# A fifth looked-up tile in the first block and one comparison for both features of a tile, in a one-core Trainium2 recommender kernel

## What is computed

```python
e = emb_tables[jnp.arange(F)[None, :], x]            # B=1024, F=32, D=64
gram = jnp.einsum('bid,bjd->bij', e, e)
cross = gram[:, iu, ju]                              # 496 pairs
h = jnp.concatenate([e.reshape(B, F * D), cross], axis=1)
h = jax.nn.relu(h @ W1 + b1)                         # 2544 -> 1024
h = jax.nn.relu(h @ W2 + b2)                         # -> 512
logits = h @ W3 + b3                                 # -> 1000
return jax.nn.sigmoid(logits)
```

## Time and profile before

| | us |
|---|---|
| median of 3 runs | 432.74 |
| lowest and highest | 430.98, 433.42 |
| the profiled execution, its own time | 431.43 |
| its span in the profile | 429.2 |
| PE busy in the span | 386.4 (90%) |
| DVE, ACT, POOL busy | 298.8, 248.0, 231.4 |

### The profile page before, as it was taken

One profiled execution on the slowest core, in us unless ns is written; L12 is line 12 of the kernel. 1 busy time (PEld: TensorE's weight loads), 2 busy tenths in 40 slices (PEclk: granted clock), 3 DMA queues, 4 the chain that ended last, 5 costly groups with the idle time before them and its releaser, 6 DMA issues.

```text
span 429.2 us, 7587 instructions
## 1 busy us (share of the span) xinstructions
PE 386.4 (90%) x2892; PEld 325.7 (76%) x2892; DVE 298.8 (70%) x568; ACT 248.0 (58%) x390; POOL 231.4 (54%) x246
## 2 busy tenths in 40 slices
PE   0887856896999998999999999999999999999996
PEld 0675744685789986788889888788889987788894
DVE  4999943484759966696579866878479767554652
ACT  3645533543667677536766676647667667444642
POOL 6887887064677777457757772457577700000000
PEclk9998898799899999999999999999999999999999
DMA  7765574069575777299874967497785864696512
GB/s 241 223 193 174 162 231 116 6 217 320 156 201 165 240 224 218 80 294 301 232 246 130 279 191 241 132 293 237 214 248 152 247 194 152 220 267 187 160 43 95
DMA packets 34451, 85.00 MB, mean 198 GB/s; under 512 B 6576, under 2 KB 13424, under 8 KB 33904
## 3 DMA queue, kind: packets, MB, share of 16 engines
q1 hardware_dynamic: 27504, 77.43, 57.1%
q0 software_dynamic: 6912, 7.09, 8.0%
HBM read 76.21 MB, written 8.29 MB: 197 GB/s over the span
## 4 chain that ended last, share of the span: by engine, by line
PE 55%; POOL 23%; issue 8%; DVE 5%; ACT 4%; DMA 3%; SPq 1%; DVEq 0%; POOLq 0%; ACTq 0%
POOL emb L429 21%; PE h1p L682 11%; PE h1p L684 11%; PE h1p L683 11%; PE misc L675 3%; PE misc L677 3%; PE misc L676 3%; PE misc L684 3%; PE misc L682 3%; PE misc L683 3%; DVE dg L587 2%; ACT wsplit L447 2%; PE misc L751 2%; POOL gap L420 2%; PE misc L729 2%
## 5 line engine op out<-in xcount | busy, mean ns | idle before, releaser
L429 POOL DMA_INDIRECT emb<-tables_dram,idx x216 | 222.3, 1029 | 112.0 <-issue 55.2
L563 DVE TENSOR_TENSOR wsplit<-wraw,wsplit 128x512 fp32r<-128x512 f32 (+1 forms) x224 | 143.7, 686 | 64.4 <-ACT wsplit L447 63.4
L447 ACT CAST wsplit<-wraw 128x1024 fp32r<-128x1024 f32 (+1 forms) x112 | 117.4, 1049 | 51.8 <-PE h1p L684 35.8
L682 PE MATMUL h1p<-wsplit,xhi 128*128 128x512 f32 x256 | 107.4, 419 | 3.6 <-DVE xlo L575 3.6
L683 PE MATMUL h1p<-wsplit,xlo 128*128 128x512 f32 x256 | 103.7, 405 | 0.0
L684 PE MATMUL h1p<-wsplit,xhi 128*128 128x512 f32 x256 | 103.6, 405 | 0.0
L682 PEld LDWEIGHTS h1p<-wsplit,xhi 128*128 128x128 f32 x256 | 50.0, 195 | 15.4 <-DVE wsplit L560 3.5
L684 PEld LDWEIGHTS h1p<-wsplit,xhi 128*128 128x128 f32 x256 | 49.9, 195 | 12.3
L683 PEld LDWEIGHTS h1p<-wsplit,xlo 128*128 128x128 f32 x256 | 50.2, 196 | 10.6
L637 DVE TENSOR_SCALAR hot<-xb,vals 128x256 fp32r<-128x256 int32 x160 | 51.9, 394 | 3.4 <-DMA xb<-xt_dram 3.4
L458 ACT COPY z<-misc 64x256 f32<-64x256 f32 x108 | 41.9, 388 | 13.8 <-DVE xlo L569 12.9
(11 more groups left out here) (50 smaller groups left out, 478.6 us busy)
## 6 DMA issues: line engine op xcount, KB each, us to landing
wraw<-w_dram SPq DMA_DIRECT2D x96, 512.0 KB, 4.6
wraw<-w_dram SPq DMA_DIRECT2D x16, 500.0 KB, 3.8
wraw<-tables_dram SPq DMA_DIRECT2D x10, 512.0 KB, 5.7
gram_scratch<-dg SPq DMA_DIRECT2D x4, 1024.0 KB, 5.0
out_dram<-res SPq DMA_DIRECT2D x16, 250.0 KB, 2.1
emb<-tables_dram,idx POOLq DMA_INDIRECT x216, 3.8
xb<-xt_dram SPq DMA_DIRECT2D x10, 256.0 KB, 5.5
gc<-gram_scratch SPq DMA_DIRECT2D x16, 64.0 KB, 4.6
```

The costliest lines, as they stand in the source:

```text
L429: nc.gpsimd.indirect_dma_start(emb[:, n % 2, k, t, f * D:(f + 1) * D], None, tables, bass.IndirectOffsetOnAxis(ap=idx[:, BT * n + t, 2 * k ...
L447: nc.scalar.copy(whi(u % RING, w), wraw[:, u % RAWS, 0:w]).then_inc(s_whi, 1)
L563: last = nc.vector.tensor_tensor(wlo(u % RING)[:, part], wraw[:, u % RAWS, part], whi(u % RING)[:, part].bitcast(fp32), ALU.subtract)
L682: nc.tensor.matmul(dst, hi, whi(slot)[:, cols], start=start, stop=False, skip_group_check=True)
```

## The change

In the first block tile 11 is looked up as well, so five tiles are looked up and eleven gathered (44 gathers instead of 48). The number of gathered tiles is then odd, and the last transpose of block 0 takes a single tile: `tiles_in(n, m)` gives one or two, and line 451, 569, 458 and 719's counterparts take half the width there. The first block's rounds are five, each with one look-up, one transpose and two emb steps, and the last transpose and emb 5 stand behind them. `products(0)` has emb 6 to 10 where it had 7 to 11. Tiles 2 and 3 of block 1 may be gathered once emb 8 of block 0 is done, not emb 11.

In all blocks the comparison is made for both features of a tile at once: eight instructions of 128x2x256 instead of sixteen of 128x256. Each of the eight signals by itself, and the look-up's products go chunk by chunk, both features of a chunk before the next chunk, each chunk waiting for its own signal. The "ones" items are therefore half as many; the one that is left stands where the first of the two stood.

```diff
-LOOKED_UP = ((12, 13, 14, 15),) + ((14, 15),) * (BLOCKS - 1)
+LOOKED_UP = ((11, 12, 13, 14, 15),) + ((14, 15),) * (BLOCKS - 1)
-        yield ("ones", 0, 1)
-        for k in range(4):
-            yield ("look", 0, 12 + k)
+        for k in range(5):
+            yield ("look", 0, 11 + k)
             yield ("tr", 0, k)
-            if k < 3:
-                yield ("ones", 0, 2 * k + 2)
-            yield from emb(0, 12 + k)
-            if k < 3:
-                yield ("ones", 0, 2 * k + 3)
-            yield from emb(0, k)
-        yield ("tr", 0, 4)
-        yield from emb(0, 4, 6)
+            if k < 4:
+                yield ("ones", 0, k + 1)
+            yield from emb(0, 11 + k, k)
         yield ("tr", 0, 5)
         yield from emb(0, 5)
...
-        yield from emb(n, *((7, 8) if n == 0 else (8,)))
+        yield from emb(n, *((6, 7) if n == 0 else (8,)))
         if more:
             yield ("ones", n + 1, 0)
-        yield from emb(n, 9)
-        if more:
-            yield ("ones", n + 1, 1)
-        yield from emb(n, 10)
+        yield from emb(n, *((8, 9) if n == 0 else (9, 10)))
         yield ("move", n)
...
-    done = (("emb", 0, 11), ("pair", 0, 0), ...
+    done = (("emb", 0, 8), ("pair", 0, 0), ...
...
+    def tiles_in(n, m):
+        return min(2, GATHERED[n] - 2 * m)
...
-                for k in range(2):
+                for k in range(tiles_in(n, m)):
...
-            def compare(h):
-                i, f = divmod(h, 2)
+            def compare(i):
                 dve.wait_ge(s_xb[i % 2], 16 * (i // 2 + 1))
-                if h >= HOTS:
-                    dve.wait_ge(s_used, used_after(*LOOKED[(h - HOTS) // 2]))
+                if i > 0:
+                    dve.wait_ge(s_used, used_after(*LOOKED[i - 1]))
                 for c in range(VC):
-                    last = nc.vector.tensor_scalar(hot[:, h % HOTS, c, :], xb[:, i % 2, f, :],
-                                                   vals[:, c:c + 1], None, ALU.is_equal)
-                last.then_inc(s_hot, 1)
+                    nc.vector.tensor_scalar(hot[:, :, c, :], xb[:, i % 2, :, :],
+                                            vals[:, c:c + 1], None, ALU.is_equal).then_inc(s_hot, 1)
...
-                for f in range(2):
-                    pe.wait_ge(s_hot, 2 * a + f + 1)
-                    for c in range(VC):
+                for c in range(VC):
+                    pe.wait_ge(s_hot, VC * a + c + 1)
+                    for f in range(2):
```

More of the change, by code:

```diff
@@ L651, in _ @@
                     looked_up_lo(n, k[0])
-                if kind == "ones" and (n, k[0]) > (0, 1):
-                    compare(2 * LOOK["look", n, LOOKED_UP[n][0]] + k[0])
+                if kind == "ones" and (n, k[0]) > (0, 0):
+                    compare(LOOK["look", n, LOOKED_UP[n][k[0]]])
                 if kind == "tr":
```

43 lines of the change are left out of this document (20 added, 23 removed).

## The result

The changed kernel takes 430.7 us in the median (20 runs, 428.28 to 434.67), the kernel before 432.64 beside it (20 runs, 430.26 to 435.62). The ratio is 0.9953, 95% interval 0.9932 to 0.9975: faster by 2.0 us, between 1.1 and 2.9. The sign was right, the size was not. The profiled execution took 430.89, its span 429.0.

What follows compares the result with a forecast made beforehand. POOL's gathers were taken to end the first block, then product reads through DRAM, then PE to bound. Terms: -7.0 at gram, +0.9 behind it, the rest 0, sum -6.1 us: 426.6 against the median 432.74, range 424.0 to 430.0.

Steps and rivals of the forecast that it cites:

- What bounds the kernel: POOL's gathers end block 0, product reads through DRAM follow, then PE bounds; earlier pair steps come off the end in full.
- Four gathers fewer: End of block 0: first 40 gathers untouched, transpose stays at 63.70, gram at 74.3 instead of 81.32, gain 7.0 us.
- The fifth look-up: Block 0's rounds: costs nothing; fifth result due at 57.9 by DVE alone, rounds of 10.0, copy must begin by 64.0.
- The wide comparison's own price: On DVE: a comparison of 512 columns takes 0.47 us, eight take 3.7, against 5.52 for a tile before.
- Behind gram: Block 0 after gram: table split and product reads issued 1.1 later; pair steps lose 0.9 us, between 0 and 2.2.
- Blocks 1 and 2: Reads there delayed by 1.2 us; block 1 has 1.75 of room and block 2 more, so cost 0.
- The two-input pace: Rival: wide comparison at two-input pace, eight take 4.9 us; gain 3.9, time 428.8; chance 0.14.
- the slower case: Rival: comparison of 512 costs at least two of 256; at 5.9 for eight, 2.6 us slower, 435.3; chance 0.06.
- POOL doesn't get faster: Rival in block 0: comparisons and gathers disturb each other, 44th gather some 6 us late; gain about 0.5, 432.2; chance 0.08.

Runs made afterwards that it cites:

- split_nogap: five_split without the small iotas that POOL runs after every two gathers of the first block; 423.06 us, ratio 0.9752 to the kernel before.
- five_split: The changed kernel with narrow comparisons of 128x256, one feature after the other at the two places as before; 427.64 us, ratio 0.9862 to the kernel before.
- experiment 5: POOL's first-block iotas, which fill a tile nothing reads, left out of the kernel before (0.9848), five_split (0.9752) and five_split with later-block wide comparisons (0.9803).
- only_five: The changed kernel with sixteen narrow comparisons at the place of the eight wide ones, iotas kept; 429.6 us, ratio 0.9896 to the kernel before.
- before_nogap: The kernel before without POOL's iotas in the first block; 425.2 us, ratio 0.9848 to the kernel before.
- hold_two: The changed kernel with SP's weight loads from emb 8 of block 0 on waiting for that block's last transpose; 430.33 us, ratio 0.9938.
- after_nogap: The changed kernel, wide comparisons everywhere they stood, without POOL's iotas in the first block; 431.21 us, ratio 0.9979 to the kernel before.
- only_cmp: The kernel before with the wide comparison alone, four tiles looked up in the first block as before; 436.35 us, ratio 1.0068 to the kernel before.
- wide_mid_nogap: The changed kernel without first-block iotas, each round's wide comparison there moved between the two emb steps; 430.07 us, ratio 0.9927 to the kernel before.
- hold: The changed kernel with SP's weight loads from emb 7 of block 0 on waiting for the transpose of tiles 8 and 9; 431.73 us, ratio 0.9950.
- before: The kernel before the change, unaltered; 432.64 us median beside the changed kernel.
- no_cmp: The changed kernel with seven of the eight comparisons of a look-up left out in four first-block rounds; 428.43 us, ratio 0.9874 to the kernel before.
- wide_mid: The changed kernel with each first-block round's wide comparison moved between its two emb steps, iotas kept; 429.25 us, ratio 0.9918 to the kernel before.

## Why the prediction was wrong in size

**What bounds the kernel** was read rightly. POOL's gathers end the first block, and every kernel here that brings gram forward and isn't held behind it is faster by about that: `split_nogap` starts gram 9.3 us earlier, and its ratio is 9.2 to 12.3 us off the total.

**Four gathers fewer** was right as a step of its own and failed on its first sentence: "The first 40 gathers are untouched ... so the transpose of tiles 8 and 9 stays at 63.70." Nothing in the program touches them; the wide comparison does, on the chip. The 40th gather is 2.5 us late, about 2 of it by gathers and iotas that run beside comparisons, and the loads that bunch behind the comparisons made its landing another 2.2 late: 4.7 of the 5.4 that gram missed. `five_split`, where the sentence holds (60.45, transpose at 63.40), gave 6.0 us. It did so with gram 4.8 earlier and not 7.0, since short waits and the low clock made 9.8 us, from one transpose to the next, of the 7.5 that the forecast had reckoned.

**The fifth look-up** at no cost came out, but not by its working. The limit was that the copy of the fifth result begins by 64.0. It begins later, on DVE's timeline of the changed kernel:

```profile
65.24 0.43 DVE L570 CAST xlo<-misc 64x256 fp32r<-64x256 f32 x1
```

PE never waits for it, because its transpose is itself at 68.39; had that stood at 63.70, PE would have waited. From the first such copy (16.70) to the fifth DVE's rounds take 12.1 us on average, not 10.0, since they follow PE, which waits for gathers. In `five_split`, where the transpose is in time, PE waits 0.78 us for the fifth copy and 1.88 for its comparisons at 61.97, and with the iotas gone as well the look-ups are what holds the block (experiment 5).

**The wide comparison's own price** was right (0.47 forecast, 0.477 measured; 3.66 for eight in a round, forecast 3.7). It was the wrong quantity to price. DVE's time isn't the bound, POOL's is, and the working costed the operation on the engine that runs it and not on the neighbour.

**Behind gram** 0.9 was reckoned and 0.4 measured (27.2 for 26.8), a term a little too large. **Blocks 1 and 2** at 0 was nearly right: the pair steps of block 1 don't wait, but PE's wait for gathered rows in block 1 grew from 1.5 to 2.4. In all eleven kernels with wide comparisons there it is 2.3 or 2.4; in those with narrow ones 1.4 to 1.8, and 2.3 in one, `only_five`.

**The rivals.** The two-input pace and the slower case fell with the 477 ns. "POOL doesn't get faster" came nearest, at 432.2 for the measured 430.7. Its price was 0.36 us on four gathers a round. Measured are 1.19 for 0.94 on one or two gathers a round, 1.43 on one in two of the rounds, and 0.12 on one or two iotas. It was held down to 0.08 by one argument: DVE spends less time comparing (3.7 for 5.5). That argument was the mistake. What counts here is how long one instruction is, not how long they are together. Over all kernels of this case 101 gathers of the first block run beside narrow comparisons alone and take 0.94 to 1.04 us, half of them 0.945 or less; 54 run beside wide ones alone and take 0.97 to 1.28, half of them 1.18 or more. The Trainium skill (SBUF — State Buffer, section "Who interferes with whom") says that an operation of this kind holds the port pair shared with GpSimd for its whole length; the direction of these runs agrees. The same section counts the two-input kind as contending with GpSimd's reads and only infers that making descriptors needs the write interface instead. Here gathers beside the splits take up to 1.48 us, and up to 4.40 when they are held to a row's end. These gathers also read their indices `idx` from SBUF, so the runs don't decide which of their phases is hindered.

The rival's own evidence was in part of another kind. No comparison runs beside the gather of 2.13 us; DVE runs this and then two splits until 68.38, 0.22 us before the gather ends:

```profile
66.33 0.91 DVE L657 MEMSET gc<- 128x1024 f32 x1 [0.16 <-issue]
```

Gathers that start inside this memset take 2.06 to 2.13 us in `before_nogap` and `hold_two` too.

**What stays open.** Which gather is held isn't settled. Those held in `after_nogap` start 0.12 to 0.81 us into a row of splits, directly behind a slow gather; in the changed kernel another starts 0.59 into one (at 62.02), behind a gather of 1.19 and an iota, and takes 0.95. The iotas don't decide it: the changed kernel has no held gather with them and five without, but `only_cmp` has them and two held gathers.

## What to carry to other kernels

Before one long VectorE instruction takes the place of two short ones, ask what GpSimd does beside it: if gathers run there and end the stage, time the gathers and not the instruction. Take such a change apart into its halves before it is judged: here one half gave 6.0 us, the other cost 2.9 where it stood alone, and the sum hid both. And filler work on the engine that ends a stage comes off the end: leaving out the iotas gave 1.5% alone and 2.5% with the fifth look-up; with wide comparisons in the first block it gave nothing (`after_nogap`) or nothing that could be told (`wide_mid_nogap`).

## What the runs showed of the hardware

- A comparison of 128x256 (int32 to fp32, 0.34 us) leaves a gather beside it at 0.94 to 1.04 us and an iota of 128x256 mostly at 0.36 (0.45 and 0.46 once each). Beside a row of comparisons of 128x512 (0.48 us each) gathers take 0.97 to 1.28 and iotas 0.48; one gather that met such a row and a split took 2.07 (`wide_mid_nogap`).
- A gather that is caught by an unbroken row of two-input instructions (128x512, 0.69 us, four to six in a row) can be held until the row is over: it ends 0.81 to 0.83 us behind it, whether it has then taken 2.17 or 4.40 us. This was seen in six of the kernels (`hold` with one of 2.17 us is among them), all but `only_five` with wide comparisons in the first block.
- How long after a gather's start its rows land goes with the load of the DMA engines meanwhile. In the waits of PE for the last rows of two tiles or one it is 2.3 to 2.5 us at a DMA share of 0.14 to 0.36 (`before`, `only_five`, `hold`), 2.9 to 3.7 at 0.51 to 0.71 (`before`, `five_split`, `hold_two`, `before_nogap`, `only_cmp`), and 4.4 to 5.8 at 0.83 to 0.92 (the changed kernel, `before_nogap`, `no_cmp`, `hold`). One falls out of this order, 4.2 at 0.52 in `wide_mid`, where the gather itself took 1.39.
